# Factorization tower: chunk 1's row traffic on ScalarE's queue, context matmuls at the start, half of chunk 0 stored early, a reordered last L2

## Chip, core and metric

One core of a Trainium2 chip. The metric is the device time of one execution in microseconds, as the median over runs. TensorE does the matmuls, VectorE and ScalarE the elementwise work and the copies out of PSUM, GpSimd part of the elementwise work and the gathers; SyncE, and here ScalarE too, issue DMAs. Matrix clock means TensorE's granted clock, 1.00 for 2.4 GHz and 0.50 for 1.2 GHz.

## The reference

512 samples, 39 fields, 16 numbers a field. A compressed interaction network of three layers of 128 maps, then a two-layer tower:

```python
e = stack([tbl_f[ids[:, f]] for f in range(39)], axis=1)      # (512, 39, 16)
x0 = xk = e
for W, b in ((w0, b0), (w1, b1), (w2, b2)):                   # W: (39, fields of xk, 128)
    z = relu(einsum('bhd,bkd,hks->bsd', x0, xk, W) + b)
    xk, direct = z[:, :64], z[:, 64:]                         # the last layer: all 128 are direct
logit = sum(concatenate(directs, axis=1), axis=-1)            # (512, 256)
h = relu(concatenate([logit, dense_ctx], axis=1) @ W_top1 + b_top1)   # 272 -> 512
h = relu(h @ W_top2 + b_top2)                                 # 512 -> 256
y = h @ W_top3
```

Everything is float32.

## The kernel before

The 512 samples are cut into 16 chunks (NCH) of 32; a chunk's columns are its 32 x 16 = 512 pairs of sample and dimension (N). For each chunk GpSimd gathers the table rows with ten indirect DMAs (GAT) into gat, four fields on 128 partitions in each; three chunks have a place in gat (GBUF). The rows are stored to a scratch tensor in DRAM, x0_dram, 39 rows of 512 numbers, in two copies by store_x0 (two DMAs a copy: nine columns of gat, and a tail), and repeated to seven copies by a DMA inside DRAM (repeat_x0). From there x0base (117 rows, load_base, three DMAs), spread0 (7 row offsets, load_spread0, for layer 0) and spread (10 groups, load_spread, in three pieces, for layers 1 and 2, two chunks' buffers) are loaded. All loads wait for the store, those of spread and spread0 for the repeat. Chunk 0's spread0 doesn't wait for the repeat: it is loaded in cuts of rows (load_first), two thirds by SyncE's queue and one third by ScalarE's, and chunk 0's second copy is stored by ScalarE (store_first_again).

A stage is one layer of one chunk: L0 has 4 groups, L1 and L2 ten. A group is an elementwise product on VectorE (product0 at line 588, product at 607) of a spread tile and the factors (base for L0, x1 for L1, x2 for L2, all in PSUM), then two matmuls into the stage's bank z0, z1 or z2. Some groups (SPLIT) are split: ScalarE rounds the product to a high part (take_high, 444), GpSimd or, for the groups in THROUGH_PSUM, VectorE subtracts it to a low part (378, 650), and TensorE does high by two weight parts (718) and low by one (733). Unsplit groups go at line 701. After L0, ScalarE writes x1 from z0 in six relu copies (relu0, line 464) and r0; after L1, x2 from z1 (relu1) and r1; after L2, r2 (relu2, 509). x1 can be written only after all products of the chunk before that read it, x2 likewise. VectorE sums r over the 16 dimensions into logits (sum01, sum2). In chunk 0 both engines share the copies (first_copies: four by ScalarE, four by VectorE).

The order is written out by hand, one stream for each engine, over the list of stages_of(i): in pass i come L0 of chunk i, the first six groups of L2 of chunk i-1 (four for the last chunk's pass), L1 of chunk i, and the rest of L2 of chunk i-1. Pass 16 has only L2 of chunk 15. Engines run their streams in order and wait on semaphores.

SyncE's queue takes the weights first, then chunk 0's store, base, cuts of spread0, repeat and three spread pieces, then the same for chunk 1 (store_x0 at 261 and 264, load_base at 283, repeat at 272, load_spread0 at 298, load_spread at 314), then the seven loads for the tower (339 to 345), then store_x0(2), and so on, one chunk for each pass. GpSimd gathers chunks 0 and 1 at its start and each later chunk two passes ahead, amid its low parts.

After pass 15 TensorE waits for the tower's weights and for z0 and z1 to be read, does the four context matmuls into h1_sum (line 763, start=True), then L2 of chunk 15 into z2 (which must have been read for chunk 14), then the matmuls of the two logit parts (769, 772), ScalarE the relu with bias from PSUM (556), TensorE the second layer (778) and the last (783), one bank of 512 columns copied out by ScalarE (563).

Of the kernel before, what the change touches and what calls it, by code (L numbers as in the profile page):

```python
# [8 lines left out]
P = 128  # L9
# [18 lines left out]
COPIES = 7  # L28

# [5 lines left out]
G0 = -(-T0 // 2)  # L35
G1 = GAT
# [107 lines left out]

def stage_end(c, kind):
    return max(DONE[c, kind, g] for g in range(G0 if kind == "L0" else G1))


def tower_kernel(nc, ids, offsets, table, w0a, w0b, w1, w1_split, w2, w2_split, biases, wt1, bt1, wt2, bt2, wt3, ctxT, out):
    with ExitStack() as ctx:  # L150
# [45 lines left out]
        y_sb = sb("y_sb", [1, B])  # L196
        h1 = spread0[:, 0:H1 // P, :]
# [8 lines left out]
        h1_sum = (z0, x1[:, 0, :], x1[:, 1, :], z1)  # L206
        h2_sum = (base, x2[:, 0, :])

# [5 lines left out]
        bias_in = sem("bias_in")  # L214
        top_in = sem("top_in")
# [4 lines left out]
        base_ready = sem("base_ready")  # L220
        spread0_first = [sem(f"spread0_first{n}") for n in range(len(FIRST_CUTS))]
# [19 lines left out]
        h1_done = sem("h1_done")  # L241
        h1_ready = sem("h1_ready")
# [9 lines left out]
        def _(sp):  # L252
            def store_x0(c, copies=(0, 1)):

                sp.wait_ge(gathered[c % GBUF], 16 * GAT * (c // GBUF + 1))
                done = x0_stored[c % 2]
                full = GAT - 1
                for n in copies:
                    at = n * F
                    first = x0_dram[c, at:at + 1, 0:1]  # L260
                    sp.dma_start(bass.AP(first.tensor, first.offset, [[D, P], [FPT * N, full], [1, D]]),
                                 gat[:, c % GBUF, 0:full, :]).then_inc(done, 16)
                    tail = x0_dram[c, at + FPT * full:at + FPT * full + 1, 0:1]
                    sp.dma_start(bass.AP(tail.tensor, tail.offset, [[D, LAST], [1, D]]),
                                 gat[0:LAST, c % GBUF, full, :]).then_inc(done, 16)

            def repeat_x0(c):

                sp.wait_ge(x0_stored[c % 2], 64 * (c // 2 + 1))
# [6 lines left out]
            def load_base(c, js=range(DPT)):  # L276

                sp.wait_ge(x0_stored[c % 2], 64 * (c // 2 + 1))
                if c >= 1:
                    sp.wait_ge(base_ready, c)  # L280
# [5 lines left out]
            def load_first(at, end, done, js):  # L286

                row = x0_dram[0, at:at + 1, 0:1]
                for j in js:
                    sp.dma_start(spread0[j * F:(j + 1) * F, at:end, :].rearrange("p t n -> p (t n)"),  # L290
                                 bass.AP(row.tensor, row.offset, [[N, F], [1, (end - at) * N]])).then_inc(done, 16)
# [47 lines left out]
            sp.dma_start(wt1_sb[:, :, :], wt1[0:2 * P, :].rearrange("(t p) n -> p t n", p=P)).then_inc(top_in, 16)  # L339
            sp.dma_start(wt1c_sb[:, :], wt1[2 * P:, :]).then_inc(top_in, 16)  # L340
            sp.dma_start(bt1_sb[:, :], bt1).then_inc(top_in, 16)
            sp.dma_start(wt2_sb[:, :, :], wt2.rearrange("(t p) n -> p t n", p=P)).then_inc(top_in, 16)
            sp.dma_start(bt2_sb[:, :], bt2).then_inc(top_in, 16)
            sp.dma_start(wt3_sb[:, :], wt3).then_inc(top_in, 16)
            sp.dma_start(ctx_sb[:, :], ctxT).then_inc(top_in, 16)
            store_x0(2)
            for i in range(1, NCH - 1):
# [5 lines left out]
                if i + 2 < NCH:  # L353
                    store_x0(i + 2)

            sp.wait_ge(y_ready, 1)
# [4 lines left out]
        def _(pool):  # L361
            def gather(c, j):

                if j == 0 and c >= GBUF:
                    old = c - GBUF
                    pool.wait_ge(x0_stored[old % 2], 64 * (old // 2 + 1))
# [4 lines left out]
                ).then_inc(gathered[c % GBUF], 16)  # L371
# [29 lines left out]
        def _(act):  # L401
# [4 lines left out]
            def store_first_again():  # L406

                act.wait_ge(gathered[0], 16 * GAT)
                first = x0_dram[0, F:F + 1, 0:1]
                act.dma_start(bass.AP(first.tensor, first.offset, [[D, P], [FPT * N, GAT - 1], [1, D]]),  # L410
                              gat[:, 0, 0:GAT - 1, :]).then_inc(x0_stored[0], 16)
                tail = x0_dram[0, F + FPT * (GAT - 1):F + FPT * (GAT - 1) + 1, 0:1]
                act.dma_start(bass.AP(tail.tensor, tail.offset, [[D, LAST], [1, D]]),
                              gat[0:LAST, 0, GAT - 1, :]).then_inc(x0_stored[0], 16)

            def load_first():

                act.wait_ge(x0_stored[0], 64)
# [4 lines left out]
                for n, (at, end) in enumerate(FIRST_CUTS):  # L423
                    row = x0_dram[0, at:at + 1, 0:1]
                    act.dma_start(spread0[j * F:(j + 1) * F, at:end, :].rearrange("p t n -> p (t n)"),
                                  bass.AP(row.tensor, row.offset, [[N, F], [1, (end - at) * N]])
# [40 lines left out]
            def first_copies(to, z, kind, layer, ready):  # L467

                act.wait_ge(mm_done, stage_end(0, kind))
# [35 lines left out]
            def relu2(c):  # L505
# [3 lines left out]
                act.activation(r2[:, :], z2[:, :], ACT.Relu, bias=bias_sb[:, 2:3]).then_inc(r2_ready, 1)  # L509
# [343 lines left out]
```

## Time and profile before

| | |
|---|---|
| median of 3 runs | 658.29 us (657.54 to 659.74) |
| the profiled execution | 657.38 us, of which the span is 655.5 us |
| TensorE busy | 608.5 us (93%) |
| VectorE busy | 550.0 us (84%) |
| GpSimd busy | 537.1 us (82%) |
| ScalarE busy | 409.3 us (62%) |
| DMA | 90.29 MB, mean 138 GB/s |

Times in the trace run from the start of the span. A profile lists for each group of instructions its busy time, its mean duration and what ended the idle time before it. A timeline row has the start, the time covered, the engine (SPq and ACTq are the DMA issues of SyncE and ScalarE), the source line, the operation, output and inputs, the count, and in brackets the idle time before it with what ended it. The landing of a DMA is counted from its issue. A busy share of TensorE says nothing of its clock, which stands in a column of its own.

### The profile page before, as it was taken

To read this page: it belongs to the slowest core of one execution; us is meant where nothing else is said; L and a number is where in the kernel's file an instruction comes from. 1 tells how busy PE (TensorE), PEld (TensorE's weight loads), DVE (VectorE), ACT (ScalarE), POOL (GpSimd) and SP (SyncE) were. 2 spreads that over 40 slices of the span, in tenths; PEclk is the share of its full clock that TensorE was granted. 3 is DMA by queue.
4 is the path that set the end of the run, shared out by engine and by line. 5 is a ranking of instruction groups with operands and counts; after the bars stand their busy time and mean duration, and the time that the engine had idled before them with its cause. 6 is when DMAs were issued, how large, how long until landed. Compare 5 with 4: busy or idle time off the path is not lost.

```text
span 655.5 us, 6276 instructions
## 1 busy us (share of the span) xinstructions
PE 608.5 (93%) x1996; PEld 376.1 (57%) x1996; DVE 550.0 (84%) x620; ACT 409.3 (62%) x551; POOL 537.1 (82%) x325
## 2 busy tenths in 40 slices
PE   0178899999999999999999999999999999999998
PEld 0035466656666566656666566666566665655563
DVE  0376899898989898998989898999989898969750
ACT  2043758677676758576766757586776667584622
POOL 6786799898989899998989998999989895746530
PEclk9979899999999999999999999999999999999999
DMA  6687883838363645648374645547383745420000
GB/s 221 150 180 222 173 249 77 250 76 248 70 209 85 167 127 130 197 82 245 71 229 91 188 90 153 160 111 216 76 250 67 213 93 176 102 64 1 0 0 0
DMA packets 64043, 90.29 MB, mean 138 GB/s; under 512 B 46624, under 2 KB 49568, under 8 KB 60042
## 3 DMA queue, kind: packets, MB, share of 16 engines
q1 hardware_dynamic: 57402, 87.89, 49.5%
q0 software_dynamic: 5120, 1.29, 2.0%
q10 hardware_dynamic: 1488, 0.72, 0.4%
q8 instruction: 15, 0.25, 0.2%
q14 instruction: 18, 0.15, 0.1%
HBM read 87.31 MB, written 8.95 MB: 147 GB/s over the span
## 4 chain that ended last, share of the span: by engine, by line
PE 40%; POOL 36%; ACT 10%; issue 6%; DVE 5%; DMA 2%; SPq 0%; ACTq 0%; DVEq 0%
POOL low L378 29%; PE z L701 21%; PE z L718 10%; POOL gat L368 7%; PE z L733 6%; ACT x L464 6%; ACT high L444 2%; DVE prod L607 2%; ACT r L488 1%; DMA spread<-x_rows 1%; DVE x L616 1%; DVE prod L588 1%; DVE base L642 1%; DVE low L650 1%; PE x L778 1%
## 5 line engine op out<-in xcount | busy, mean ns | idle before, releaser
L378 POOL TENSOR_TENSOR low<-prod,high 128x1024 fp32r<-128x1024 f32 (+1 forms) x160 | 380.9, 2398 | 56.4 <-ACT high L444 55.1
L607 DVE TENSOR_TENSOR prod<-spread,x 128x1024 f32<-128x1024 f32 x256 | 308.1, 1214 | 35.3 <-ACT x L464 33.6
L701 PE MATMUL z<-prod,w_sb 128*128 128x512 f32 (+2 forms) x608 | 290.6, 598 | 37.3 <-DVE prod L588 32.8
L444 ACT ACTIVATE high<-prod 128x1024 fp32r<-128x1024 f32 (+1 forms) x160 | 167.8, 1058 | 124.0 <-DVE prod L607 99.8
L718 PE MATMUL z<-high,high_w_L 128*128 128x512 f32 (+1 forms) x448 | 203.7, 455 | 4.0 <-ACT high L444 2.8
L701 PEld LDWEIGHTS z<-prod,w_sb 128*128 128x128 f32 (+2 forms) x608 | 115.4, 190 | 122.8 <-issue 103.4
L368 POOL DMA_INDIRECT gat<-table_dram,index x160 | 155.5, 972 | 36.5 <-issue 33.9
L733 PE MATMUL z<-low,high_w_L 128*128 128x512 f32 (+1 forms) x448 | 182.1, 487 | 3.5 <-POOL low L378 1.9
L718 PE MATMUL z<-high,low_w_L 128*128 128x512 f32 (+1 forms) x448 | 179.0, 400 | 0.0
L464 ACT ACTIVATE x<-z,bias_sb 64x512 f32<-64x512 f32 (+1 forms) x180 | 116.3, 646 | 14.8 <-PE z L701 7.4
L733 PEld LDWEIGHTS z<-low,high_w_L 128*128 128x128 f32 (+1 forms) x448 | 82.8, 190 | 68.9 <-issue 44.7
L454 ACT ACTIVATE high<-base 128x512 fp32r<-128x512 f32 x128 | 75.5, 590 | 55.6 <-DVE base L642 55.2
L718 PEld LDWEIGHTS z<-high,high_w_L 128*128 128x128 f32 (+1 forms) x448 | 85.5, 191 | 42.2 <-issue 14.4
L718 PEld LDWEIGHTS z<-high,low_w_L 128*128 128x128 f32 (+1 forms) x448 | 85.5, 191 | 31.8 <-issue 14.2
L650 DVE TENSOR_TENSOR low<-base,high 128x512 fp32r<-128x512 f32 x128 | 87.8, 686 | 8.6 <-ACT high L454 8.3
L642 DVE TENSOR_TENSOR base<-spread,x 128x512 f32<-128x512 f32 x128 | 88.6, 692 | 2.3
L588 DVE TENSOR_TENSOR prod<-spread,base 117x1024 f32<-117x1024 f32 x64 | 65.4, 1082 | 15.0 <-DMA spread<-x_rows 8.4
L509 ACT ACTIVATE r<-z,bias_sb 128x512 f32<-128x512 f32 x16 | 11.0, 687 | 13.8 <-PE z L733 13.7
L628 DVE TENSOR_REDUCE logit<-r 128x32 f32<-128x512 f32 x16 | 10.9, 679 | 7.4 <-ACT r L509 7.4
L435 ACT ACTIVATE base<-x0base 117x512 f32<-117x512 f32 x16 | 9.6, 602 | 8.6 <-DMA x0base<-x_rows 8.2
L656 DVE TENSOR_TENSOR low_w_L<-spread,high_w_L 128x1792 fp32r<-128x1792 f32 (+1 forms) x2 | 3.7, 1888 | 10.1 <-DMA gat<-table_dram,index 10.1
L488 ACT ACTIVATE r<-z,bias_sb 64x512 f32<-64x512 f32 x16 | 11.0, 686 | 0.4
(37 smaller groups left out, 73.5 us busy)
## 6 DMA issues: line engine op xcount, KB each, us to landing
spread<-x_rows SPq DMA_DIRECT2D x15, 1792.0 KB, 7.1
spread<-x_rows SPq DMA_DIRECT2D x32, 768.0 KB, 11.0
spread<-x_rows SPq DMA_DIRECT2D x16, 1024.0 KB, 7.3
x_rows<-x_rows SPq DMA_DIRECT2D x16, 390.0 KB
x0base<-x_rows SPq DMA_DIRECT2D x47, 78.0 KB
gat<-table_dram,index POOLq DMA_INDIRECT x160, 3.7
x_rows<-gat SPq DMA_DIRECT2D x31, 72.0 KB, 2.3
wt_sb<-wt_dram SPq DMA_DIRECT2D x2, 512.0 KB, 17.4
```

What stands on the lines that cost most here:

```text
L368: pool.indirect_dma_start(out=gat[0:rows, c % GBUF, j, :], out_offset=None, in_=table, in_offset=bass.IndirectOffsetOnAxis(ap=index[0:rows ...
L378: pool.tensor_tensor(low[0:rows, h, 0:k, :], prod[0:rows, slot(c, kind, g), 0:k, :], high[0:rows, h, 0:k, :].bitcast(F32), ALU.subtract).t ...
L444: act.activation(high[0:rows, split_slot(c, kind, g), 0:k, :], prod[0:rows, slot(c, kind, g), 0:k, :], ACT.Copy).then_inc(high_ready, 1)
L454: act.activation(high[0:rows, split_slot(c, kind, g), t, :], base[0:rows, :], ACT.Copy).then_inc(tile_high, 1)
L464: act.activation(to[at:end, tile, :], z[k:k + end - at, :], ACT.Relu, bias=bias_sb[k:k + end - at, layer:layer + 1]).then_inc(ready, 1)
L588: dve.tensor_tensor(prod[0:rows, slot(c, "L0", g), 0:k, :], spread0[0:rows, 2 * g:2 * g + k, :], base[0:rows, :].unsqueeze(1).to_broadcast ...
L607: dve.tensor_tensor(prod[0:rows, slot(c, kind, g), :, :], spread[0:rows, c % 2, g, :].unsqueeze(1).to_broadcast([rows, k, N]), x[0:rows, : ...
L642: dve.tensor_tensor(base[0:rows, :], spread[0:rows, c % 2, g, :], x[0:rows, t, :], ALU.mult).then_inc(tile_prod, 1)
L650: dve.tensor_tensor(low[0:rows, h, t, :], base[0:rows, :], high[0:rows, h, t, :].bitcast(F32), ALU.subtract).then_inc(tile_low, 1)
L701: last = pe.matmul(z[:, :], w[0:rows, at + j, :], prod[0:rows, slot(c, kind, g), j, :], start=g == 0 and j == 0, stop=closes and j == k - 1)
L718: pe.matmul(z[:, :], v[kind][0:rows, at + j, :], high[0:rows, h, j, :], start=g == 0 and j == 0 and v is high_w, stop=False)
L733: last = pe.matmul(z[:, :], high_w[kind][0:rows, at + j, :], low[0:rows, h, j, :], start=False, stop=closes and j == k - 1)
```

## The change

It has these parts:

- **Chunk 1.** Its stores, repeat, base loads and spread0 load leave SyncE's queue and are issued by ScalarE: store_x0(1, (0, 1)) and repeat_second() right after its last L0 operation in pass 0, ahead of its x1 copies; load_second() after those and r0. Chunk 1's three spread pieces stay with SyncE, directly after chunk 0's.
- **Half of chunk 0.** The first five gathers (SOON) count on a semaphore of their own. Their rows are stored as soon as they are there (store_soon, and the second copy by ScalarE), and load_soon loads the first 13 rows of each third of spread0 from them. The later store and cuts cover the rest: five columns fewer, 26 rows in place of 39.
- **Context matmuls.** Their three small loads are issued right behind the biases. TensorE does the four context matmuls before everything else, into x1 and x2; VectorE adds the bias to each into ctx_part in SBUF. In the tower the matmul of the first logit part starts the sum, VectorE adds ctx_part into h1, and ScalarE does the relu in place.
- **Last L2.** L2 of chunk 15 goes into z0, not z2, so it waits for r0 instead of r2. Its x2 copies are shared by both engines (shared_copies). ScalarE does r2 of chunk 14 after group 2 of it, VectorE its sum after group 5 instead of 3.
- **Tower loads.** Four of them are issued after pass 4's loads. The last layer is computed and copied out in two halves of columns.

```diff
@@
+TOP_AT = 4
+SOON = 5
...
+SOON_ROWS = SOON * FPT - T0
...
+def gathers_until(c):
+    return 16 * (GAT * (c // GBUF + 1) - (SOON if c % GBUF == 0 else 0))
+
+def stored_until(c):
+    return 64 * (c // 2 + 1) + (16 if c % 2 == 0 else 0)
...
-        h1_sum = (z0, x1[:, 0, :], x1[:, 1, :], z1)
+        h1_sum = (z2, x1[:, 0, :], x1[:, 1, :], z1)
+        ctx_sum = (x1[:, 0, :], x1[:, 1, :], x2[:, 0, :], x2[:, 1, :])
+        y_sum = (z0[0:1, 0:B // 2], z1[0:1, 0:B // 2])
+        def sum_bank(c, kind):
+            return z0 if kind == "L2" and c == NCH - 1 else {"L0": z0, "L1": z1, "L2": z2}[kind]
...
@@ SyncE
+            def store_soon():
+                sp.wait_ge(gathered_soon, 16 * SOON)
+                first = x0_dram[0, 0:1, 0:1]
+                sp.dma_start(bass.AP(first.tensor, first.offset, [[D, P], [FPT * N, SOON], [1, D]]),
+                             gat[:, 0, 0:SOON, :]).then_inc(stored_soon, 16)
+            def load_soon():
+                sp.wait_ge(stored_soon, 16)
+                row = x0_dram[0, 0:1, 0:1]
+                for j in range(DPT):
+                    sp.dma_start(spread0[j * F:j * F + SOON_ROWS, :, :].rearrange("p t n -> p (t n)"),
+                                 bass.AP(row.tensor, row.offset, [[N, SOON_ROWS], [1, T0 * N]])
+                                 ).then_inc(spread0_soon, 16)
...
             sp.dma_start(bias_sb[:, :], biases).then_inc(bias_in, 16)
+            sp.dma_start(wt1c_sb[:, :], wt1[2 * P:, :]).then_inc(ctx_in, 16)
+            sp.dma_start(ctx_sb[:, :], ctxT).then_inc(ctx_in, 16)
+            sp.dma_start(bt1_sb[:, :], bt1).then_inc(ctx_in, 16)
...
+            store_soon()
+            load_soon()
             store_x0(0, (0,))
...
-            store_x0(1)
-            load_base(1)
-            repeat_x0(1)
-            load_spread0(1)
             for p in range(len(PIECES)):
                 load_spread(1, p)
...
@@ ScalarE
+            def store_x0(c, copies):
+                if c == 0:
+                    act.wait_ge(gathered_soon, 16 * SOON)
...
+                act.wait_ge(gathered[c], gathers_until(c))
...
+            def repeat_second():
+                act.wait_ge(x0_stored[1], stored_until(1))
...
+            def load_second():
+                for j in range(DPT):
+                    row = x0_dram[1, (F - j * T0) % F:(F - j * T0) % F + 1, 0:1]
+                    act.dma_start(x0base[j * F:(j + 1) * F, :], bass.AP(row.tensor, row.offset, [[N, F], [1, N]])
+                                  ).then_inc(base_in, 16)
+                act.wait_ge(prod_done, PROD_NUMBER[0, "L0", G0 - 1])
+                act.wait_ge(x0_copied[1], 16)
...
-            store_first_again()
+            store_x0(0, (1,))
             load_first()
             take_base(0)
             for i in range(NCH + 1):
-                if i >= 2:
+                if i == NCH:
+                    shared_copies(i - 1, x2, z1, "L1", 1, x2_ready)
+                    relu1(i - 1, 2)
+                elif i >= 2:
                     for part in range(3):
                         relu1(i - 1, part)
-                if i == NCH:
-                    relu2(NCH - 2)
...
+                        if i == NCH and g == 2:
+                            relu2(i - 2)
...
                     if kind == "L0" and i == 0:
-                        first_copies(x1, z0, "L0", 0, x1_ready)
+                        store_x0(1, (0, 1))
+                        repeat_second()
+                        shared_copies(0, x1, z0, "L0", 0, x1_ready)
                         relu0(i, 2)
+                        load_second()
...
@@ VectorE
+            dve.wait_ge(ctx_in, 16 * 3)
+            for m in range(H1 // P):
+                dve.wait_ge(ctx_done, m + 1)
+                dve.tensor_scalar(ctx_part[:, m, :], ctx_sum[m], bt1_sb[:, m:m + 1], 0.0, ALU.add, ALU.add)
...
             for i in range(NCH + 1):
+                if i == NCH:
+                    shared_copies(i - 1, x2, z1, "L1", 1, x2_ready)
...
             sum2(NCH - 1)
+            for m in range(H1 // P):
+                dve.wait_ge(h1_done, m + 1)
+                dve.tensor_tensor(h1[:, m, :], h1_sum[m][:, :], ctx_part[:, m, :], ALU.add).then_inc(h1_summed, 1)
...
@@ TensorE
-                if gs[0] == 0 and c >= 1:
+                if kind == "L2" and c == NCH - 1 and gs[0] == 0:
+                    pe.wait_ge(r0_ready, NCH)
+                elif gs[0] == 0 and c >= 1:
...
+            pe.wait_ge(ctx_in, 16 * 3)
+            for m in range(H1 // P):
+                pe.matmul(ctx_sum[m], wt1c_sb[:, m * P:(m + 1) * P], ctx_sb[:, :],
+                          start=True, stop=True).then_inc(ctx_done, 1)
             pe.wait_ge(w1_in, 32)
...
```

## Rows read from the trace of the kernel before

**Rows 1.** One steady pass, busy time by engine (count), TensorE clock, DMA share, GB/s
```profile
118.21:154.56 36.35, 36.20 (x123) 22.80 (x123) 33.65 (x39) 25.13 (x34) 33.35 (x21) 1.00 0.60 166
```
**Rows 2.** Timeline of TensorE, the first L1 matmul and L1 of chunk 1
```profile
42.65 3.78 PE L701 MATMUL z<-prod,w_sb 128*128 128x512 f32 x4 [4.55 <-DVE prod L607]
...
84.33 0.74 PE L733 MATMUL z<-low,high_w_L 128*128 128x512 f32 x2 [1.27 <-POOL low L378]
```
**Rows 3.** Timeline of VectorE, passes 0 and 1
```profile
38.21 3.13 DVE L616 TENSOR_SCALAR x<-z,bias_sb 32x512 f32<-32x512 f32 x4 [3.31 <-PE z L701]
41.37 2.35 DVE L607 TENSOR_TENSOR prod<-spread,x 128x1024 f32<-128x1024 f32 x2
...
61.94 4.08 DVE L588 TENSOR_TENSOR prod<-spread,base 117x1024 f32<-117x1024 f32 x4 [6.28 <-issue]
...
69.21 2.35 DVE L607 TENSOR_TENSOR prod<-spread,x 128x1024 f32<-128x1024 f32 x2
```
**Rows 4.** Timeline of ScalarE, pass 0
```profile
38.14 2.65 ACT L472 ACTIVATE x<-z,bias_sb 32x512 f32<-32x512 f32 x4 [4.55 <-PE z L701]
...
56.79 0.60 ACT L435 ACTIVATE base<-x0base 117x512 f32<-117x512 f32 x1
```
**Rows 5.** Timeline of SyncE's issues, chunks 0 and 1
```profile
34.05 1.88 SPq L314 DMA_DIRECT2D spread<-x_rows  x3
...
51.35 0.85 SPq L272 DMA_DIRECT2D x_rows<-x_rows  x1
55.16 0.34 SPq L298 DMA_DIRECT2D spread<-x_rows  x1
```
**Rows 6.** The chain that ended last, in order of time: the stores of chunk 0
```profile
19.04 3.05 DMA x_rows<-gat
```
**Rows 7.** One gather, last two spread pieces (chunk 0); the page's median store
```profile
L368 POOL DMA_INDIRECT gat<-table_dram,index x1: 974/974/974, 36.2 to 36.2; - x1
DMA to landing us min/median/max: 9.1/9.1/9.1
...
L314 SPq DMA_DIRECT2D spread<-x_rows x2: 590/594/597, 34.7 to 35.3; - x2
DMA to landing us min/median/max: 8.9/11.0/13.1
...
x_rows<-gat SPq DMA_DIRECT2D x31, 72.0 KB, 2.3
```
**Rows 8.** Line 368 alone: the tenth gather of chunk 1
```profile
L368 POOL DMA_INDIRECT gat<-table_dram,index x1: 918/918/918, 30.9 to 30.9; - x1
DMA to landing us min/median/max: 3.7/3.7/3.7
```
**Rows 9.** Timelines of ScalarE, VectorE and TensorE, the last pass and the end
```profile
611.68 4.01 ACT L464 ACTIVATE x<-z,bias_sb 64x512 f32<-64x512 f32 x6 [0.72 <-DVE prod L607]
...
615.72 2.35 DVE L607 TENSOR_TENSOR prod<-spread,x 128x1024 f32<-128x1024 f32 x2 [4.12 <-ACT x L464]
...
617.06 1.12 PE L763 MATMUL z<-ctx_sb,wt1c_sb 16*128 16x512 f32 x2
...
622.52 0.63 PE L718 MATMUL z<-high,low_w_L 128*128 128x512 f32 x1
...
636.72 1.03 PE L733 MATMUL z<-low,high_w_L 128*128 128x512 f32 x2
...
653.34 0.59 ACT L563 ACTIVATE y_sb<-z 1x512 f32<-1x512 f32 x1 [1.12 <-PE z L783]
```
**Rows 10.** Groups of instructions on the page: busy us, mean ns, idle before and releaser
```profile
L378 POOL TENSOR_TENSOR low<-prod,high 128x1024 fp32r<-128x1024 f32 (+1 forms) x160 | 380.9, 2398 | 56.4 <-ACT high L444 55.1
...
L444 ACT ACTIVATE high<-prod 128x1024 fp32r<-128x1024 f32 (+1 forms) x160 | 167.8, 1058 | 124.0 <-DVE prod L607 99.8
```
**Rows 11.** Timelines of SyncE and VectorE, chunk 5's spread0 and its products
```profile
224.74 0.36 SPq L298 DMA_DIRECT2D spread<-x_rows  x1
...
245.63 4.08 DVE L588 TENSOR_TENSOR prod<-spread,base 117x1024 f32<-117x1024 f32 x4
```

More of the change, by code:

```diff
@@ L286, in load_first @@
             def load_first(at, end, done, js):
-                row = x0_dram[0, at:at + 1, 0:1]
+                row = x0_dram[0, SOON_ROWS + at:SOON_ROWS + at + 1, 0:1]
                 for j in js:
-                    sp.dma_start(spread0[j * F:(j + 1) * F, at:end, :].rearrange("p t n -> p (t n)"),
-                                 bass.AP(row.tensor, row.offset, [[N, F], [1, (end - at) * N]])).then_inc(done, 16)
+                    sp.dma_start(spread0[j * F + SOON_ROWS:(j + 1) * F, at:end, :].rearrange("p t n -> p (t n)"),
+                                 bass.AP(row.tensor, row.offset, [[N, F - SOON_ROWS], [1, (end - at) * N]])
+                                 ).then_inc(done, 16)
             def load_spread0(c):
@@ L404, in split_weights @@
                                ).then_inc(high_w_ready, 1)
[L406 to L414, printed above, removed]
+            def store_x0(c, copies):
+                if c == 0:
+                    act.wait_ge(gathered_soon, 16 * SOON)
+                    soon = x0_dram[0, F:F + 1, 0:1]
+                    act.dma_start(bass.AP(soon.tensor, soon.offset, [[D, P], [FPT * N, SOON], [1, D]]),
+                                  gat[:, 0, 0:SOON, :]).then_inc(x0_stored[0], 16)
+                act.wait_ge(gathered[c], gathers_until(c))
+                skip = SOON if c == 0 else 0
+                for n in copies:
+                    first = x0_dram[c, n * F + FPT * skip:n * F + FPT * skip + 1, 0:1]
+                    act.dma_start(bass.AP(first.tensor, first.offset, [[D, P], [FPT * N, GAT - 1 - skip], [1, D]]),
+                                  gat[:, c, skip:GAT - 1, :]).then_inc(x0_stored[c], 16)
+                    at = n * F + FPT * (GAT - 1)
+                    tail = x0_dram[c, at:at + 1, 0:1]
+                    act.dma_start(bass.AP(tail.tensor, tail.offset, [[D, LAST], [1, D]]),
+                                  gat[0:LAST, c, GAT - 1, :]).then_inc(x0_stored[c], 16)
@@ L465, in copies, with shared_copies @@
                                    bias=bias_sb[k:k + end - at, layer:layer + 1]).then_inc(ready, 1)
[L467 to L469 removed]
+            def shared_copies(c, to, z, kind, layer, ready):
+                act.wait_ge(mm_done, stage_end(c, kind))
+                if c >= 1:
+                    ringed, tiled = products_of(c - 1, "L1" if kind == "L0" else "L2", range(G1))
+                    act.wait_ge(prod_done, ringed)
+                    if tiled:
+                        act.wait_ge(tile_prod, tiled)
                 for tile in range(2):
@@ L561, in _ @@
                                bias=bt2_sb[:, m:m + 1]).then_inc(h2_ready, 1)
-            act.wait_ge(y_done, 1)
-            act.activation(y_sb[:, :], z0[0:1, :], ACT.Copy).then_inc(y_ready, 1)
+            for n in range(2):
+                act.wait_ge(y_done, n + 1)
+                act.activation(y_sb[:, n * B // 2:(n + 1) * B // 2], y_sum[n], ACT.Copy).then_inc(y_ready, 1)
         @block.vector
@@ L595, in wait_factors @@
                 if g == 0:
-                    dve.wait_ge(ready, (2 + FPT) * (c + 1) + 2)
+                    dve.wait_ge(ready, (2 + FPT) * (c + 1) + (4 if kind == "L2" and c == NCH - 1 else 2))
                 for p, (at, _) in enumerate(PIECES):
@@ L609, in product, with shared_copies @@
                                   x[0:rows, :, :], ALU.mult).then_inc(prod_done, 1)
-            def first_copies(to, z, kind, layer, ready):
-                dve.wait_ge(mm_done, stage_end(0, kind))
+            def shared_copies(c, to, z, kind, layer, ready):
+                dve.wait_ge(mm_done, stage_end(c, kind))
+                if c >= 1:
+                    ringed, tiled = products_of(c - 1, "L1" if kind == "L0" else "L2", range(G1))
+                    dve.wait_ge(prod_done, ringed)
+                    if tiled:
+                        dve.wait_ge(tile_prod, tiled)
                 for tile in range(2):
@@ L757, in _ @@
                     sum_stage(c, kind, gs)
-            pe.wait_ge(top_in, 16 * 7)
-            pe.wait_ge(r0_ready, NCH)
-            pe.wait_ge(r1_ready, NCH)
-            for m in range(H1 // P):
-                pe.matmul(h1_sum[m][:, :], wt1c_sb[:, m * P:(m + 1) * P], ctx_sb[:, :], start=True, stop=False)
             for c, kind, gs in stages_of(NCH):
                 sum_stage(c, kind, gs)
+            pe.wait_ge(top_in, 16 * 4)
+            pe.wait_ge(r2_ready, NCH - 1)
+            pe.wait_ge(r1_ready, NCH)
             pe.wait_ge(summed01, NCH)
             for m in range(H1 // P):
-                pe.matmul(h1_sum[m][:, :], wt1_sb[:, 0, m * P:(m + 1) * P], logit01[:, :], start=False, stop=False)
+                pe.matmul(h1_sum[m][:, :], wt1_sb[:, 0, m * P:(m + 1) * P], logit01[:, :], start=True, stop=False)
             pe.wait_ge(summed2, NCH)
@@ L782, in _ @@
                 pe.wait_ge(h2_ready, k + 1)
-                last = pe.matmul(z0[0:1, :], wt3_sb[:, k:k + 1], h2[:, k, :],
-                                 start=(k == 0), stop=(k == H2 // P - 1))
-            last.then_inc(y_done, 1)
+                for n in range(2):
+                    last = pe.matmul(y_sum[n], wt3_sb[:, k:k + 1], h2[:, k, n * B // 2:(n + 1) * B // 2],
+                                     start=(k == 0), stop=(k == H2 // P - 1))
+                    if k == H2 // P - 1:
+                        last.then_inc(y_done, 1)
 def layer_rows(w, gs):
```

91 lines of the change are left out of this document (56 added, 35 removed).

## The prediction

> **What bounds the kernel now.** I began with a steady pass of the loop. TensorE is busy 36.20 of 36.35 us there and VectorE 33.65 [rows 1], so from the second pass on TensorE sets the pace and only work taken out of its stream, or idle time taken away, shortens the span. The change takes nothing out of passes 2 to 15. Next I looked for TensorE's gaps. The start has several, from 4.55 us before the first L1 matmul of chunk 0 to 1.27 in L1 of chunk 1; after 84.33 none of size follows until the last pass [rows 2]. So the kernel is a start, fourteen rigid passes of 36.3 us, and a tail. A shift of the start arrives whole at the end, a tail gain adds to it.
>
> Which chain sets the start? VectorE's rows [rows 3] and ScalarE's [rows 4]: z0 is done at 38.1, the two engines copy x1 out of it (four copies of VectorE 3.13 us, four of ScalarE 2.65), the first L1 product begins at 41.37. After the last one VectorE stands idle 6.28 us to 61.94. The queue of SyncE says why [rows 5]: chunk 1's spread0 load is issued at 55.16, because its store stands in that queue behind the three pieces of chunk 0's spread (first issue 34.05), and the repeat could go only at 51.35. The four L0 products, the x2 copies and the first L2 product (69.21) follow without a gap.
>
> Call T the start of the first L1 product and D the landing of spread0 for chunk 1. base for chunk 1 is ready 57.40 − 41.37 = 16.0 us after T (56.79 + 0.60, [rows 4]), the four L0 products and the copies take 69.21 − 61.94 = 7.3, so the first L2 product comes at the later of T + 16.0 + 7.3 = T + 23.3 and D + 7.3. Before: 64.7 and 69.2, D decides. After it the passes follow by ScalarE's relu, VectorE and GpSimd, whose first low part ends TensorE's 1.27 us gap in L1 of chunk 1 [rows 2]; that TensorE runs eight matmuls at half clock just before (below) is absorbed there. So **the shift of the start is max(T + 23.3, D + 7.3) − 69.2**.
>
> **Part 1, the early half of chunk 0.** Five gathers' rows (20 fields) are stored and spread amid the rest. The stores of both copies took 3.05 us from issue to landing before [rows 6]. The rest that is left is smaller, but the early load, 3 × 13 rows × 14 KB = 546 KB, is ahead of it in SyncE's queue. I cost the landing at no change (22.1), bounds −0.8 (the 2.3 us of SyncE's median store [rows 7] in place of 3.05) and +1.5. What is behind it does shrink: base, spread0 and the repeat were 2.26 MB from 22.1 to the release of the pieces at 34.05 [rows 5]; now 1.72 MB. At the same rate (11.9 us less about 2 of latency for 2.26 MB, so 9.9 × 0.54/2.26 = 2.4 us saved) the pieces go out at about **31.6**. The first cuts save a share of that, 1.5 us for z0, so z0 is done at 36.6. A gain only if the copies can start then.
>
> **Part 2, chunk 1 by ScalarE's queue.** This is where I expect the gain of part 1 and more to go. After its last L0 operation ScalarE waits for chunk 1's ten gathers, issues four stores, waits for them to land (repeat_second), issues the repeat, and only then does its x1 copies. Everything behind those two waits stands: four x1 copies, r0, then load_second with its own wait, and the high parts of L1. VectorE's own four copies don't wait, but its first L1 product does, for both.
> The tenth gather is issued at 30.86, 0.92 us long, and landed 3.7 us after [rows 8]; with lighter traffic around it, ScalarE issues from about 34.0. By then the three pieces of chunk 0's spread (2.56 MB) have been issued, at 31.6 to 33.5, on the other queue. What does a small transfer from another queue do there? The nearest row is the gather issued at 36.2 amid the same pieces: it landed 9.1 us later, where the median store takes 2.3, and the last piece itself 13.1 after its issue at 35.33 [rows 7]. A gather moves 128 rows of 64 B; the two copies of the store are 18 times that. I take it that the store lands with or just behind the last piece: pieces out at 31.6, the last landed 35.33 + 13.1 − 34.05 = 14.4 later, 46.0, and 0.6 for what is left of the store: **landing 46.6**. Bounds: 38.0 (34.0, 1.7 of issue, 2.3), and 49.
> The DMA page of the Trainium skill (DMA: Bandwidth & Descriptors, Queues, rings and completion order) says that each DMA engine takes turns between the queues at packet granularity, so that small rows wait their turn behind large ones; by that rule the store cannot pass the pieces either. Its section Issuing engines are not separate DMA queues puts it against this change: another issuing engine saves only sequencer time. The 9.1 us row agrees with both.
> From the landing: repeat's issue 0.85 (SyncE's price, [rows 5]), ScalarE's four copies 2.65, handoffs 0.1, so T = 46.6 + 3.6 = 50.2, 8.8 later than 41.37. D: the repeat took 3.8 us before (51.35 to 55.16), so it lands at about 51, ScalarE issues spread0 at about 52, next to the pieces of chunk 1 on the other queue. Landing took 6.7 us for it with its queue to itself (55.16 to 61.9 [rows 3, 5]) and at worst all 4.35 MB before it are shared, 14 us: D between 59 and 66, and T + 16.0 = 66.2. D no longer decides. The 6.28 us gap is gone, as the change means it to be, but T is later by more:
> shift of the start = 50.2 + 23.3 − 69.2 = **+4.3 us**; with the bounds of the landing 38.0 and 49, −4.3 (T 41.6) and +6.7. Even is at a landing of 42.3.
>
> **Part 3, the tail.** Before, copies of x2 for chunk 15 took ScalarE alone 4.01 us, 611.68 to 615.69, VectorE starting its first last product at 615.72; TensorE filled the time with 3.6 us of context matmuls (617.06 to 620.69) and then ran about 3.2 us at half clock (rows of 0.63 in place of 0.40 us) [rows 9]. After: shared copies cost VectorE 3.13 us [rows 3], the first product 614.8, its high part about 617.1, which is just when TensorE ends L2 of chunk 14. It writes z0, so it needn't wait for r2. L2 of chunk 15 thus starts 3.6 us earlier; with the half clock gone too (3.2 us at 2.4 GHz are 1.6) the most is 5.2. But VectorE is only 0.95 ahead: going through the ten groups with 1.2 us a product [rows 3], 1.1 a high part, 2.4 a low part [rows 10], the second tiles of groups 2 and 6 make TensorE wait about 1 us each and the end comes near 634.5 in place of 637.76 [rows 9]. **−3.3 us**, bounds −1.5 and −5.2. The add of the context part on VectorE (0.7 a block) stands between the h1 matmuls and the relu; the first h2 matmul starts only when all four blocks' matmuls are through, and needs the fourth block 2.6 us after, against 1.5 for add and relu: nothing. If that cover failed it would cost 0.7. The output copy in two halves: half of 0.59 [rows 9], −0.2.
>
> **Edits costed at nothing.** Context matmuls first: about 7.5 us cold, from about 8, with VectorE's four adds after them by 16.7, while it otherwise waits for chunk 0's gathers, as the stores issued at 19.04 do [rows 6]; if the loads come 3 us late they would push the low weights by 1. They end long before the first L0 matmul, so they don't warm it. Top loads moved to pass 4: 1 MB, four issues, on a queue that issues spread0 at 224.74 for products at 245.63 [rows 11]: less 7 for the load, 13 us of slack, some 5 used.
>
> **Sum.** +4.3 − 3.3 − 0.2 = +0.8 us on the profiled execution's 657.38, which lies 0.9 below the median of 658.29. On medians: **659.1**, own range 656.5 to 662.
>
> **The rivals.**
> (a) The store isn't held: ScalarE's queue is served at once, in the 2.3 us of the median store [rows 7]. Landing 38.0, start −4.3 (if spread0 lands by 57.6), total −7.8: **650.5**. For it: all DMA engines are shared evenly by the cuts of both queues before 33 us. Against: the gather's 9.1. Chance 0.14.
> (b) The store is held, but gets through between the second and third piece, at about 43: start +0.7, total −2.8: **655.5**, and 654 with a somewhat better tail. By the skill's turns at packets this is the outcome if a turn takes several of its small rows. Chance 0.22.
> (c) Slower: the gathers of chunk 1 themselves are caught. The pieces now go out before the tenth gather has landed; if it takes the 9.1 us of [rows 7] it lands at about 41, the four stores are issued by 43.4 and land behind the pieces at 49: start +6.7, total +3.2 or, with the tail at its lower bound, +5: **661.5 to 663**. It decides once the pieces' first data precede the tenth gather's landing by 1 us. Chance 0.17.
> (d) The forecast. Chance 0.47.
>
> **How the numbers follow.** 0.3% is 2.0 us, about what a measurement of this kernel can tell: faster is under 656.3, slower over 660.3. Faster: all of (a), most of (b), little of (d), 0.35. Slower: (c) and a fifth of (d), 0.26. Same: 0.39. The range, 651.0 to 662.5, leaves out most of (a) and the end of (c).
>
> **What would show it.** ScalarE's x1 copies at 47 to 50 with VectorE's at 37 to 40; TensorE idle some 13 us after L0 of chunk 0; no gap on VectorE before L0 of chunk 1; L1 of chunk 1 starting at 84 instead of 80; TensorE unbroken from L2 of chunk 14 into that of chunk 15, at full clock. I am wrong if the x1 copies start before 43, or if TensorE waits over 2 us in the last L2.

## The result and the profile after

| | median | ratio to before (95%) |
|---|---|---|
| before | 658.85 us | |
| changed kernel | 662.13 us | 1.0064 (1.0048 to 1.0079) |

Each stands on 9 runs. The change costs 0.64%, or 4.2 us by the ratio; the two medians are 3.3 us apart. The profiled execution went from 657.38 to 661.98 us, its span from 655.5 to 660.2: 4.7 us more. That is a start that arrives 8.2 us later at the end of chunk 14's L2 and a tail that is 3.5 us shorter.

The start, timelines of ScalarE (ACTq: its DMA issues), VectorE and TensorE after:

```profile
18.24 0.45 ACTq L463 DMA_DIRECT2D x_rows<-gat  x1
25.21 0.62 ACTq L497 DMA_DIRECT2D x0base<-x_rows  x1
...
35.48 0.41 ACTq L463 DMA_DIRECT2D x_rows<-gat  x1
...
37.85 5.47 ACTq L467 DMA_DIRECT2D x_rows<-gat  x1
50.75 0.90 ACTq L475 DMA_DIRECT2D x_rows<-x_rows  x1
51.70 0.64 ACT L553 ACTIVATE x<-z,bias_sb 32x512 f32<-32x512 f32 x1 [16.28 <-DMA x_rows<-gat]
...
40.57 3.13 DVE L710 TENSOR_SCALAR x<-z,bias_sb 32x512 f32<-32x512 f32 x4 [4.48 <-PE z L804]
54.38 2.35 DVE L696 TENSOR_TENSOR prod<-spread,x 128x1024 f32<-128x1024 f32 x2 [10.68 <-ACT x L553]
...
70.43 4.08 DVE L677 TENSOR_TENSOR prod<-spread,base 117x1024 f32<-117x1024 f32 x4 [1.75 <-ACT base L511]
...
77.70 2.35 DVE L696 TENSOR_TENSOR prod<-spread,x 128x1024 f32<-128x1024 f32 x2
...
55.65 3.78 PE L804 MATMUL z<-prod,w_sb 128*128 128x512 f32 x4 [15.19 <-DVE prod L696]
```

Read ScalarE's row of 51.70 first: 16.28 us of idle time, ended by the landing of a store. VectorE had made its own four x1 copies from 40.57 to 43.70; its first product waits until 54.38 for the other four. TensorE's gap, 4.55 us in [rows 2], is 15.19. The gap of 6.28 us on VectorE ahead of chunk 1's L0 products [rows 3] is down to 1.75, and it is base, no longer a DMA, that ends it. The first L2 product is at 77.70 in place of 69.21, 8.5 us late. From there the kernels run alike but for 0.3 us: chunk 14's L2 ends 8.2 us late (625.36 and 617.13).

Before, the same four stores stood in SyncE's queue behind the same pieces (issued from 34.05, [rows 5]); the base loads in the last row were waiting for them:

```profile
36.86 5.94 SPq L264 DMA_DIRECT2D x_rows<-gat  x1
...
43.37 4.64 SPq L264 DMA_DIRECT2D x_rows<-gat  x1
50.17 1.13 SPq L283 DMA_DIRECT2D x0base<-x_rows  x3
```

They landed at 50.2 there and at 50.7 on ScalarE's queue, so the move gained nothing in time of landing. The long issues, 5.94 and 4.64 us, were in the trace of before too, on an engine without compute work; the prediction allowed 1.7 us for all four on ScalarE.

SyncE's queue after, where the three pieces of chunk 0 begin the last row:

```profile
14.54 0.38 SPq L295 DMA_DIRECT2D x_rows<-gat  x1
16.60 1.14 SPq L303 DMA_DIRECT2D spread<-x_rows  x3
18.23 0.39 SPq L285 DMA_DIRECT2D x_rows<-gat  x1
18.66 0.50 SPq L288 DMA_DIRECT2D x_rows<-gat  x1
25.21 0.72 SPq L327 DMA_DIRECT2D x0base<-x_rows  x2
...
35.30 21.32 SPq L359 DMA_DIRECT2D spread<-x_rows  x6
```

Chunk 0's remaining rows are stored from 18.23, the last by ScalarE at 18.72, and landed at 25.2, 6.5 us after that last issue, where 3.05 us sufficed for all of them [rows 6]. So the pieces go out at 35.30, later than the 34.05 of before [rows 5].

The end, timelines of VectorE, TensorE and ScalarE after:

```profile
619.94 3.13 DVE L710 TENSOR_SCALAR x<-z,bias_sb 32x512 f32<-32x512 f32 x4
623.10 2.35 DVE L696 TENSOR_TENSOR prod<-spread,x 128x1024 f32<-128x1024 f32 x2
...
625.56 0.47 PE L821 MATMUL z<-high,high_w_L 128*128 128x512 f32 x1 [0.20 <-ACT high L520]
...
629.91 0.50 PE L821 MATMUL z<-high,high_w_L 128*128 128x512 f32 x1 [0.79 <-ACT high L530]
...
641.61 1.03 PE L836 MATMUL z<-low,high_w_L 128*128 128x512 f32 x2
...
657.80 0.80 ACT L650 ACTIVATE y_sb<-z 1x256 f32<-1x256 f32 x2 [0.70 <-PE z L891]
```

The last L2 starts 0.20 us after that of chunk 14 and has one wait of 0.79; no matmul of it runs at half clock. Its end went from 637.76 to 642.64: 4.9 us later where chunk 14's L2 ends 8.2 later, so 3.3 gained. Another 0.2 is gained behind it.

### The profile page after: what moved, and what is told of

Same layout as the page of the kernel before. It is cut to its first block and busy times, and to the rows that moved or that the text cites. A ratio compares the mean times of both kernels' runs of the same rounds, so it can differ in the third digit from the quotient of the medians.

```text
span 660.2 us, 6306 instructions
## 1 busy us (share of the span) xinstructions
PE 608.9 (92%) x2000; PEld 374.9 (57%) x2000; DVE 558.9 (85%) x632; ACT 408.1 (62%) x550; POOL 534.8 (81%) x325
## 5 line engine op out<-in xcount | busy, mean ns | idle before, releaser
L696 DVE TENSOR_TENSOR prod<-spread,x 128x1024 f32<-128x1024 f32 x256 | 308.1, 1214 | 41.6 <-ACT x L540 15.2
L414 POOL DMA_INDIRECT gat<-table_dram,index x160 | 153.5, 960 | 36.6 <-issue 34.3
L821 PE MATMUL z<-high,low_w_L 128*128 128x512 f32 (+1 forms) x448 | 177.2, 396 | 0.0
L540 ACT ACTIVATE x<-z,bias_sb 64x512 f32<-64x512 f32 (+1 forms) x174 | 112.5, 646 | 13.8 <-PE z L804 7.4
L821 PEld LDWEIGHTS z<-high,high_w_L 128*128 128x128 f32 (+1 forms) x448 | 84.5, 189 | 41.8 <-issue 14.5
L553 ACT ACTIVATE x<-z,bias_sb 32x512 f32<-32x512 f32 x12 | 7.7, 642 | 17.2 <-DMA x_rows<-gat 16.3
L859 PE MATMUL x<-ctx_sb,wt1c_sb 16*128 16x512 f32 x8 | 7.2, 1076 | 7.9 <-DMA bt_sb<-bt_dram 7.9
```

What stands on the lines that cost most here:

```text
L414: pool.indirect_dma_start(out=gat[0:rows, c % GBUF, j, :], out_offset=None, in_=table, in_offset=bass.IndirectOffsetOnAxis(ap=index[0:rows ...
L540: act.activation(to[at:end, tile, :], z[k:k + end - at, :], ACT.Relu, bias=bias_sb[k:k + end - at, layer:layer + 1]).then_inc(ready, 1)
L696: dve.tensor_tensor(prod[0:rows, slot(c, kind, g), :, :], spread[0:rows, c % 2, g, :].unsqueeze(1).to_broadcast([rows, k, N]), x[0:rows, : ...
L821: pe.matmul(z[:, :], v[kind][0:rows, at + j, :], high[0:rows, h, j, :], start=g == 0 and j == 0 and v is high_w, stop=False)
```

## The experiments

Two rival accounts of the loss: ScalarE's traffic is held by chunk 0's spread pieces and its copies wait for it (with the early half adding a little of its own), or the early half upsets both queues and chunk 1 on ScalarE's queue would be fine alone. The first three runs take the two start parts apart; all keep the tail and context edits.

**Neither start part.** No early half (SOON is 0), and chunk 1's rows by SyncE in the order of before:

```diff
-            store_soon()
-            load_soon()
...
+            store_x0(1)
+            load_base(1)
+            repeat_x0(1)
+            load_spread0(1)
             for p in range(len(PIECES)):
                 load_spread(1, p)
...
-                        store_x0(1, (0, 1))
-                        repeat_second()
                         shared_copies(0, x1, z0, "L0", 0, x1_ready)
                         relu0(i, 2)
-                        load_second()
```

> The changed kernel without its two start parts: chunk 0 isn't stored early, and chunk 1's rows go by SyncE's queue as before. Left are the context matmuls at the start, the last L2, the tower loads of pass 4 and the split output. Theory (the parts add, the loss is all in the start): the start stays as before, first L2 product at 69.2, and the end gains 3.7 us: ratio to before 0.9944. Rival (the early context matmuls or the tower loads cost something that the shift of the start hides): ratio 0.998 to 1.000, with a first L0 product later than 28.4 or a gap of TensorE in pass 5 or 6.

Measured: 654.68 us, 0.9946 (0.9927 to 0.9966). First L2 product 69.56. The tail alone is worth 3.6 us, as forecast. The first L0 product came at 28.87, later than the rival's 28.4, but the first L1 product at 41.21 was not late (41.37 before), so the context matmuls at the start cost nothing that can be measured.

**The early half alone** (as above, with store_soon and load_soon kept):

> As the kernel without both start parts, but with the early half of chunk 0. Theory (the early load ahead of the rest's store in the queue delays it by 3 us, which costs chunk 0 1.3 us at the issue of its pieces, and chunk 1 by SyncE's queue follows them): first L1 product about 43.7, spread0 of chunk 1 landed at 63.2 instead of 61.9, start +1.3, ratio 0.9964. Rival (the store is late in the changed kernel only because of ScalarE's part of the traffic): chunk 0's stores land at 22, start -2, ratio 0.991.

Measured: 655.99 us, 0.9963 (0.9947 to 0.998). The rest's stores were issued at 19.09 and landed at 25.3, the pieces went out at 35.53. So it is not ScalarE's chunk 1 that delays them. The first L2 product moved from 69.56 to 72.14, 2.6 us where 1.3 was expected. The medians differ by 1.3 us only, and so do the spans of the profiled executions, 653.4 and 654.7. For the spans the reason is in the trace: both kernels have a gap of TensorE of 1.3 us in L1 of chunk 1, but only the one with neither start part ran at half clock behind it (granted clock 0.50 from 86 to 88 us, 0.95 over the pass).

```profile
84.65 0.91 PE L836 MATMUL z<-low,high_w_L 128*128 128x512 f32 x2 [1.28 <-POOL low L426]
```

From there to the first matmul behind chunk 14's L2 it took 534.1 us, the kernel before 532.7 and the changed one 532.8. For the medians, which lie as close, the runs don't show a reason. So a difference of these ratios is good to about 1 us, and not better; the 3 us on the landing stand by themselves.

**Chunk 1 by ScalarE alone** (the changed kernel without the early half):

> As the kernel without both start parts, but with chunk 1 by ScalarE's queue. Theory (the store on ScalarE's queue lands 15.4 us after the issue of chunk 0's pieces, behind them, and ScalarE's x1 copies wait for it): pieces issued at 34.05, landing 49.4, first L1 product at 53.1, start +7.2, with the tail +3.5 us, ratio 1.0053. Rival (it was the early half that disturbed ScalarE's store): landing before 40, start -3 to 0, ratio 0.990 to 0.9945.

Measured: 661.02 us, 1.0037 (1.0021 to 1.0052). ScalarE and SyncE:

```profile
34.26 21.16 SPq L359 DMA_DIRECT2D spread<-x_rows  x6
...
34.67 0.39 ACTq L461 DMA_DIRECT2D x_rows<-gat  x1
...
36.64 6.02 ACTq L465 DMA_DIRECT2D x_rows<-gat  x1
49.55 0.90 ACTq L473 DMA_DIRECT2D x_rows<-x_rows  x1
50.50 0.64 ACT L552 ACTIVATE x<-z,bias_sb 32x512 f32<-32x512 f32 x1 [16.92 <-DMA x_rows<-gat]
```

Landing at 49.5, 15.2 us after the pieces' issue (15.4 in the changed kernel), first L1 product at 53.18 against 53.1. The expected ratio was 1.0053, a little above the interval. The four ratios make a square:

| | chunk 1 by SyncE | by ScalarE |
|---|---|---|
| no early half | 0.9946 | 1.0037 |
| early half | 0.9963 | 1.0064 |

ScalarE's queue costs 0.9 to 1.0%, some 6 us; the early half 0.2 to 0.3%, 1 to 2 us (the intervals of its two pairs overlap; at the first L2 product it costs 2.6 us in one pair and 1.2 in the other, in one profile each); the tail returns 0.5%.

**Copies ahead of the wait.** Is it the wait, or chunk 1's data?

```diff
                         store_x0(1, (0, 1))
-                        repeat_second()
                         shared_copies(0, x1, z0, "L0", 0, x1_ready)
                         relu0(i, 2)
+                        repeat_second()
                         load_second()
```

> The changed kernel with ScalarE's x1 copies and r0 moved ahead of the wait for chunk 1's store (the stores are still issued ahead of them). Theory (the loss is ScalarE standing at the wait, not the late store itself): copies at 43.3, when the last store's issue ends, first L1 product at 46.0; the wait then holds the high parts of L1 until about 51.6, so the products end some 4.4 us earlier than in the changed kernel; ratio to before 1.000. Rival (chunk 1's data set the start): same as the changed kernel, 1.0064.

Measured: 660.90 us, 1.004 (1.0027 to 1.0053), between theory (1.000) and rival (1.0064). The first product came at 45.94 as expected; what it gained went to the next wait:

```profile
43.26 2.65 ACT L553 ACTIVATE x<-z,bias_sb 32x512 f32<-32x512 f32 x4 [7.91 <-issue]
...
50.54 0.90 ACTq L475 DMA_DIRECT2D x_rows<-x_rows  x1
...
54.64 0.37 ACTq L488 DMA_DIRECT2D spread<-x_rows  x1
55.06 1.06 ACT L520 ACTIVATE high<-prod 128x1024 fp32r<-128x1024 f32 x1 [8.44 <-DMA x_rows<-x_rows]
```

ScalarE stood 8.44 us, until the repeat had landed as well, ahead of the first high part of L1. I had counted the wait for the store only and left out load_second's own (3.5 us). Of 8.4 us less before the first product 6.7 were lost again at the high parts.

**The stores ahead of the early load.** Starting from the kernel with the early half alone:

```diff
             store_soon()
-            load_soon()
             store_x0(0, (0,))
+            load_soon()
```

> The kernel with the early half of chunk 0 and chunk 1 by SyncE's queue, with one order turned: SyncE issues the store of chunk 0's rest ahead of the early spread0 load instead of behind it. Theory (the early load in the queue ahead holds the store: issue to landing was 6 us with it, 3.2 without): the store lands about 3 us after its issue at 18.8, near 22, the pieces of spread go out at 32.5 to 33.5 instead of 35.5, ratio to before 0.992 to 0.9945. Rival (splitting the store in two is what makes it late, or the early load disturbs it wherever it is issued): landing at 24 to 25, ratio 0.9955 to 0.997.

Measured: 655.54 us, 0.9957 (0.9939 to 0.9976). The store landed at 19.99, 2.5 us after its issue at 17.51, so the early load ahead of it was what held it. But base, behind the early load now, was issued at 19.99 and ready only at 27.18; 2.8 us had been enough without the early load (21.29 to 24.05 with neither start part). The first L0 product came at 29.43, no earlier than the 28.87 with neither start part, and the ratio stayed short of the expected 0.992 to 0.9945. The delay moved one place down. DMA over the stretch, here and with neither start part (the last two columns are the DMA share and GB/s):

```profile
22.00:26.00 4.00, 0.00 (x0) 0.00 (x0) 0.00 (x0) 0.00 (x0) 2.85 (x4) 1.00 0.77 113
```
```profile
22.00:26.00 4.00, 0.00 (x0) 0.00 (x0) 0.00 (x0) 0.60 (x1) 3.05 (x4) 1.00 0.81 228
```

With the early load among the traffic, half the bytes move with the DMA engines about as busy. These stretches hold base rows and cuts too; the changed kernel has the early load nearly alone, from 17.0 to 21.5 us, at 131 GB/s and a DMA share of 0.93. Its 546 KB thus take about 4.5 us (4.4 to 4.8 at the 113 to 123 GB/s of the early-half kernels), not the 2.4 that the 228 GB/s would give.

**The pieces held back.** Does the spread of chunk 0 hold ScalarE's store?

```diff
+            sp.wait_ge(x0_stored[1], stored_until(1))
             for p in range(len(PIECES)):
                 load_spread(0, p)
```

> The changed kernel, except that SyncE issues chunk 0's three spread pieces only when chunk 1's store on ScalarE's queue has landed. Theory (the pieces hold the store): with nothing large beside it the store lands within 5 us of its first issue, before 41, ScalarE's x1 copies start at 40.5 to 41.5 instead of 51.7; the first product then waits for the first piece, which lands 6.5 us after its issue, at 46 to 47; start 1 to 2 us later than before, ratio 0.996. Rival (the store is slow on ScalarE's queue whatever lies beside it): landing after 47, ratio 1.006 or more, since the pieces come late as well.

Measured: 657.06 us, 0.9982 (0.9964 to 1.0001). ScalarE in the profile:

```profile
35.55 0.39 ACTq L464 DMA_DIRECT2D x_rows<-gat  x1
35.98 0.62 ACTq L468 DMA_DIRECT2D x_rows<-gat  x1
36.63 0.45 ACTq L464 DMA_DIRECT2D x_rows<-gat  x1
37.10 0.63 ACTq L468 DMA_DIRECT2D x_rows<-gat  x1
39.21 0.90 ACTq L476 DMA_DIRECT2D x_rows<-x_rows  x1
41.84 0.64 ACT L554 ACTIVATE x<-z,bias_sb 32x512 f32<-32x512 f32 x1 [6.76 <-PE z L837]
```

Landed 3.7 us after the first issue instead of 15.3, no issue longer than 0.63 us, and the x1 copies wait for z0 alone. That settles it: the store on ScalarE's queue waits for SyncE's pieces. VectorE then waited 0.61, 1.65 and 0.88 us for the late pieces, and the expected ratio, 0.996, lies just below the interval. The gather of chunk 0 ended late in this profile (21.8), and z0 with it (41.8), so its start isn't compared.

**Only the issues on ScalarE.** The kernel with neither start part, with chunk 1's four stores alone given to ScalarE ahead of its copies, nothing waiting there:

> The kernel without both start parts (tail and context edits only), with nothing but chunk 1's four store issues moved to ScalarE, ahead of its x1 copies; repeat, base and spread0 stay with SyncE behind the pieces. There is no wait on the store's landing on ScalarE any more. Theory (ScalarE still stands in the issue of the last store until the queue has room, 6 us, and the store lands at 49 whichever queue takes it): ScalarE's copies start at 42.7, T = 45.3, T + 23.3 = 68.6; spread0 of chunk 1 at 61 to 62, D + 7.3 = 69: start as before, ratio 0.9945. Rival (the issue is free without the wait): T 41.3, and D earlier because the store starts sooner, ratio 0.990.

Measured: 653.09 us, 0.9922 (0.9895 to 0.9948). The last issue took 5.91 us (36.75 to 42.66) and the copies began at 42.71, T = 45.39, store landed at 49.8, first L2 product 69.11: every step as the theory has it. The ratio can't be told from 0.9946.

**Another order for SyncE's queue.** The same formula says where time can be had: chunk 1's spread0 must land by T + 16. Three orders were tried, each from the kernel with neither start part: chunk 1's store ahead of chunk 0's pieces; behind the first piece; behind the second.

```diff
-            for p in range(len(PIECES)):
-                load_spread(0, p)
-            store_x0(1)
-            load_base(1)
-            repeat_x0(1)
+            load_spread(0, 0)
+            load_spread(0, 1)
+            store_x0(1)
+            load_spread(0, 2)
+            repeat_x0(1)
+            load_base(1)
             load_spread0(1)
```

> The kernel without both start parts (tail and context edits only), SyncE's queue in another order: chunk 1's store, then chunk 0's first piece, chunk 1's repeat, the other two pieces, chunk 1's base and spread0. By T + 23.3 and D + 7.3: the first piece is issued at 36.3 instead of 33.6 and lands at 43, T = 43; spread0 of chunk 1 lands at 57 to 59 instead of 62. The later is 66.3: start -2.9, total -6.5 us, ratio 0.990. Rival (the total of bytes decides, in whatever order): spread0 lands at 61 to 62 as before, ratio 0.9945.

> As the kernel with chunk 1's store first in SyncE's queue, but with chunk 0's first piece ahead of the store, the second behind it, then chunk 1's repeat, the third piece, base and spread0. T stays 41.2; the store lands behind the first piece at 40 to 41, the repeat goes out then, spread0 of chunk 1 at 47 and lands at 56 to 58. Start T + 23.3 = 64.5, -4.6 us, total -8.2 us, ratio 0.9875, if the third piece (issued at 42, landing about 50) is there for its group at 50. Rival (the third piece is late): a gap of VectorE in L1 of chunk 0 and ratio 0.990 to 0.993.

> As the kernel with chunk 1's store second in SyncE's queue, but with chunk 0's first two pieces ahead of the store, then the store, the third piece, and only then chunk 1's repeat, base and spread0. The two kernels before had gaps of VectorE of 1.9 to 2.2 us for the second piece. Theory (the start is max(T + 23.3, D + 7.3), T without a gap in L1): T 41.3, no gap, the repeat lands behind the third piece at 50.5, spread0 at 57.5, first L2 product 64.8, total -8 us, ratio 0.988. Rival (the store behind two pieces is late enough for the repeat to slip): spread0 at 60, first L2 product 67.3, ratio 0.9915, no better than the others.

Measured: 654.28 us, 0.993 (0.9906 to 0.9954); 653.55 us, 0.9921 (0.9892 to 0.995); and 650.73 us, **0.9889** (0.9862 to 0.9916). In the first, T was 43.01 as expected, and in both the second piece then came late by 1.9 to 2.2 us (VectorE's wait before 47.98 and before 47.03), so both fell short of the expected 0.990 and 0.9875; the second came out as its rival of a late piece said. With two pieces ahead VectorE has only a wait of 0.71 us, for a piece, before 50.65. VectorE of the third:

```profile
41.56 2.35 DVE L697 TENSOR_TENSOR prod<-spread,x 128x1024 f32<-128x1024 f32 x2
...
58.46 4.08 DVE L678 TENSOR_TENSOR prod<-spread,base 117x1024 f32<-117x1024 f32 x4 [1.81 <-ACT base L515]
...
65.74 2.35 DVE L697 TENSOR_TENSOR prod<-spread,x 128x1024 f32<-128x1024 f32 x2
```

First L2 product 65.74 (64.8 expected), ratio 0.988 expected and 0.9889 measured. This kernel beats both the kernel before, by 1.1%, and the changed one, and its interval lies clear of the 0.9946 (0.9927 to 0.9966) of the usual order; from the other two orders the intervals don't separate it.

## Why the prediction was right or wrong

It said 659.1 with no measurable change as the likeliest (0.39), and 0.26 for slower; the loss is 4.2 us where 0.8 was forecast. The time of 662.13 lies inside the range, near its upper end.

- **Where the start comes from: right.** max(T + 23.3, D + 7.3) gives 77.7 for the measured T = 54.38; the trace has 77.70. It held in the variants as well. Where T decides: ScalarE's queue alone, T = 53.18, gives 76.5 (76.50 measured). Where D decides: with neither start part D = 62.29 gives 69.6 (69.56), with the early half alone D = 64.87 gives 72.2 (72.14). Chunk 1's store first: T = 43.01 and the 1.9 us at the second piece give 68.2 (68.3). The fastest kernel, T = 41.56 and D = 51.34 + 7.0 = 58.3, gives 65.6 by D (65.74). For the two with D = 62.29 and 64.87, D is read as the start of the product that waits for it, so they test the 7.3 alone.
- **Part 2, the mechanism and its distance: right.** The store was to land 15.0 us behind the issue of the pieces; it did so after 15.4 and, alone, 15.2. Holding the pieces back made it 3.7. Rivals (a) and (b) are refuted by this. The Trainium skill's turns between queues at packets (DMA: Bandwidth & Descriptors, Queues, rings and completion order) fit a store of small rows that lands with or after three large transfers, but no run here tests them: before, in one queue with the pieces, the store landed 16.1 us behind their issue, nearly the same, and how many rows go in a turn no run shows.
- **Part 1, the landing of chunk 0's store: wrong, and it is the step that failed.** "I cost the landing at no change (22.1), bounds −0.8 … and +1.5." It landed at 25.2, +3.1, outside these bounds. The prediction named the early load as ahead of the store in the queue and gave it no price: the delay was put at nothing. It took the DMA engines about 4.5 us, and with the order turned the store landed in 2.5. From this come 3.1 of the 3.7 us by which the pieces went out late (35.3 in place of 31.6); the other 0.6 is base, cuts and repeat, 10.1 us in place of 9.5. With the pieces T came at 54.4 in place of 50.2, and the shift of the start at 8.5 in place of 4.3. Put 25.2 for 22.1 into the prediction's own sum and it gives 659.1 + 3.1 = 662.2.
- **Rival (c)** gave nearly the time that came, 661.5 to 663, but by another road. The tenth gather wasn't caught: ScalarE's issues began at 35.48, not 41. Its chance went to the right side for the wrong reason.
- **The issue of the stores: missed, without effect here.** 1.7 us was allowed for ScalarE's four issues; the last one alone took 5.47. It lay hidden under the wait for the landing. Without that wait it sets T, at 45.39 (only the issues on ScalarE).
- **The tail: right.** −3.3 for L2 and −0.2 for the output; 3.3 and 0.2 measured, −3.6 with the tail alone. The end of L2 was to be 634.5 with an unshifted start; 642.64 less 8.2 is 634.4. Of the two waits of TensorE of about 1 us one came, 0.79. The add stands hidden: h2's matmuls begin as L879 ends.
- **Costed at nothing: right.** The context matmuls took 7.19 us from 7.89 and VectorE's adds ended at 15.9, before the last of chunk 0's gathers had landed (18.2).
- **The signs.** ScalarE's copies came at 51.7 (47 to 50 named), TensorE's idle time was 15.2 us (13 named), and VectorE kept a gap of 1.75 us before L0 of chunk 1 where none was named; each is off to the side of a later start. The tail ran unbroken but for waits of 0.20 and 0.79 us, at full clock, as named.
- **The weighing.** With bounds of −0.8 to +1.5 on the landing my own range of the forecast ended at 662. The chance for slower should have held the case that an added transfer delays the small one queued behind it, which SyncE's queue had shown already for chunk 1: its store stands behind large pieces there.

## What to carry to other kernels

A store of many small rows should be queued before large loads, or after just as many of them as the engines need next; giving it to another engine's queue didn't get it past them here, and a wait for its landing on an engine with compute work stops that work too. Before moving a DMA to a compute engine, list what stands behind each of its issues and waits there; here they were the x1 copies and then the high parts. The early partial load paid in neither order tried: ahead of the store it delayed the store, behind the store it delayed base. Price such a load, at its own measured rate, against what stands behind it in the queue.

## What the runs showed of the hardware

- A DMA issue is not always short. The last of ScalarE's four store issues took 5.47, 6.02, 5.50 and 5.91 us with SyncE's pieces in flight, and 0.63 with them held back; where no wait for the landing stood ahead of them, ScalarE's next copies started only then (43.26, 42.71). SyncE's own issues of the same stores behind the pieces took 5.94 and 4.64 before, and with the stores ahead of the pieces at most 0.60. The Trainium skill (DMA: Bandwidth & Descriptors, Issuing engines are not separate DMA queues) says that a second issuing engine saves sequencer time; here it moved that time from SyncE, which does no compute work, to ScalarE, whose copies stood behind it.
- Stretches with the early load's three DMAs (13 rows of 14 KB each, one partition a row) moved 113 to 131 GB/s with a DMA share of 0.77 to 0.93, those with the cuts of 39 rows of 4 to 6 KB 207 to 228 GB/s, those with cuts of 26 rows 206 to 214. Whether it is the number of rows and so of partitions written, their length, or reading what was just written, no run tells: it stays open.
- TensorE's clock. Before, the last L2 ran some 3 us at half clock, right after the 16-row context matmuls [rows 9]; after, without them in between, all of 626 to 643 was granted 1.00, with waits of up to 0.79 us. Other half-clock stretches stand in the start, before for instance from 72 to 75 us; the one behind 84.65 in the kernel with neither start part goes with a stretch of passes 1.3 us longer than in the others.
